# First edge attention of a four-layer graph network: the gathers of every fourth item wait for PE's shift of the maxima

## What is computed

```python
attn_score = jnp.sum(aw_q_edge * k[row_idx], axis=-1)      # one score for each edge and head
m = jax.ops.segment_max(score, col_idx, num_segments=n)
ex = jnp.exp(score - m[col_idx])
...
agg = jax.ops.segment_sum(alpha[..., None] * msg_edge, col_idx, num_segments=n)
```

## Time and profile before

| | |
|---|---|
| three runs | 6724.58, 6731.64, 6753.25 us; median 6731.64 us |
| span of the profiled execution, first to last instruction | 6706.8 us |
| its own time outside of the profiler | not given; the median of the runs lies 24.8 us above the span |
| busy: PE, DVE, POOL, ACT | 4342.6, 3458.5, 3192.9, 2184.9 us |
| first edge attention (l0e) | from about 619 to about 2280 us of the span |
| second edge attention (l3e) | from about 4884 to about 6572 us |

### The profile page before, as it was taken

The page is one execution under the profiler, slowest core; times in us unless marked ns, Lnnn a source line. Parts: engine busy times, 40 slices in busy tenths (PEclk is TensorE's granted clock), DMA queues, the critical chain, the costliest instruction groups (busy, mean ns, idle before and its releaser), DMA issues. The chain is left out here.

```text
span 6706.8 us, 90264 instructions
## 1 busy us (share of the span) xinstructions
PE 4342.6 (65%) x24913; PEld 3150.9 (47%) x24913; DVE 3458.5 (52%) x6689; ACT 2184.9 (33%) x7656; POOL 3192.9 (48%) x3187
## 2 busy tenths in 40 slices
PE   6996676766677744544444546887646666666676
PEld 4664454544445423333333435766335555555553
DVE  4452666666666662211111231112558888888885
ACT  1221455555545430000000111222225454555541
POOL 0422566666666236676676520002145565655551
PEclk8896777777777876666766778998778888888885
DMA  4334666666666525333333407882366666666673
GB/s 133 126 123 163 182 197 199 202 196 198 198 196 197 125 72 186 93 93 93 92 95 92 72 29 243 261 262 87 108 189 205 203 210 203 205 207 203 201 185 102
DMA packets 509932, 1077.03 MB, mean 161 GB/s; under 512 B 94770, under 2 KB 322388, under 8 KB 505993
## 3 DMA queue, kind: packets, MB, share of 16 engines
q0 software_dynamic: 204144, 617.42, 32.6%
q1 hardware_dynamic: 296854, 452.03, 20.2%
q10 hardware_dynamic: 8512, 2.74, 0.2%
HBM read 964.49 MB, written 194.54 MB: 173 GB/s over the span
## 5 line engine op out<-in xcount | busy, mean ns | idle before, releaser
L772 POOL DMA_INDIRECT l0e_kv<-t_table,k_recs x912 | 986.1, 1081 | 636.9 <-ACT l0e_vw L1049 375.5
L772 POOL DMA_INDIRECT l3e_kv<-t_table,k_recs x912 | 971.0, 1065 | 667.5 <-ACT l3e_vw L1049 368.0
L1464 PE MATMUL l2e_pA<-l2e_row,l2e_oh 128*128 128x257 f32 x1824 | 633.4, 516 | 768.7 <-issue 380.4
L1418 POOL DMA_INDIRECT l2e_row<-t_table,l2e_idx x912 | 899.7, 986 | 389.7 <-issue 265.4
L1464 PEld LDWEIGHTS l2e_pA<-l2e_row,l2e_oh 128*128 128x128 f32 x1824 | 460.0, 262 | 942.0 <-issue 852.9
L1006 PE MATMUL l0e_pA<-l0e_vw,l0e_ohf 128*128 128x260 f32 x1824 | 643.9, 500 | 198.3 <-ACT l0e_vw L1049 129.2
L958 PE MATMUL l3e_pQE<-l3e_qb,l3e_ohT 128*128 128x256 bf16 x2736 | 428.0, 318 | 405.9 <-issue 378.7
L1049 ACT ACTIVATE l3e_vw<-l3e_kv,l3e_w 128x64 f32<-128x64 f32 x2736 | 679.8, 334 | 0.0
L1049 ACT ACTIVATE l0e_vw<-l0e_kv,l0e_w 128x64 f32<-128x64 f32 x2736 | 679.6, 334 | 0.0
L1443 DVE SCALAR_TENSOR_TENSOR l2e_acc<-l2e_acc,k_itf,l2e_pA 128x257 f32<-128x257 f32 x228 | 109.9, 482 | 1058.6 <-issue 981.9
L1006 PEld LDWEIGHTS l0e_pA<-l0e_vw,l0e_ohf 128*128 128x128 f32 x1824 | 427.7, 247 | 338.5 <-ACT l0e_vw L1049 156.6
(11 more groups left out here) (469 smaller groups left out, 7126.8 us busy)
## 6 DMA issues: line engine op xcount, KB each, us to landing
exp_w<-in_L_gnn_w SPq DMA_DIRECT2D x224, 512.0 KB
t_table<-l0n_tab SPq DMA_DIRECT2D x26, 2048.0 KB, 6.9
l0e_qb<-t_q SPq DMA_DIRECT2D x228, 192.0 KB
l3e_qb<-t_q SPq DMA_DIRECT2D x228, 192.0 KB
t_agg<-l0e_acc SPq DMA_DIRECT2D x228, 130.0 KB
t_agg<-l3e_acc SPq DMA_DIRECT2D x228, 130.0 KB
l0e_drow<-t_drow SPq DMA_DIRECT2D x57, 512.0 KB
l3e_drow<-t_drow SPq DMA_DIRECT2D x57, 512.0 KB
```

Of the source, the lines that this page charges most:

```text
L772: pool.indirect_dma_start(kv[:, n % SK, g, :], None, table[:, :], bass.IndirectOffsetOnAxis(ap=K["recs"][:, n, g, ridx:ridx + 1], axis=0)) ...
L1418: pool.indirect_dma_start(row[:, s, g, 0:D], None, table[:, :], bass.IndirectOffsetOnAxis(ap=idx[:, i, g:g + 1], axis=0)).then_inc(row_rea ...
L1464: last = pe.matmul(pA[s % 2][:, 0:W], oh[:, s, g, :], row[:, s, g, :], start=(g == 0), stop=(g == G - 1))
```

## The change

Before the gathers of item n POOL gets one more wait, in the first edge attention alone, when n is 1 modulo 4 and over 8, so for n = 9, 13, ..., 225 (55 items):

```diff
                 if n >= SK:
                     pool.wait_ge(vwa_ready, n - SK + 1)
                     pool.wait_ge(vwd_ready, n - SK + 1)
+                if first and n % BI == 1 and n > 2 * BI:
+                    pool.wait_ge(sh_ps, (n - 1) // BI - 1)
                 for g in range(G):
```

## The result

The changed kernel is slower: 6857.62 us (6835.46 to 6870.38, four runs) against 6731.00 us of the kernel before beside it, a ratio of 1.0174 with a 95% interval of 1.0146 to 1.0202. By the ratio that is 117 us more, by the two medians 127 us, where 198 us less were forecast.

The account below looks back on a forecast made before the run. Bursts were taken as bound by PE's shift report, held until gathers drain. Release 0.1, 16 gathers 21.2, drain 3.0 and PE 0.3 make 24.6 us against 28.27, over 54 periods 198 us: 6731.6 - 198 = 6533 us, range 6463 to 6750.

Parts of the forecast that it names:

- What bounds the kernel: First edge attention: PE's report of the shift, awaited by `z`, is held while gathers stream; a burst takes 28.27 us.
- From report to last gather before the next hold this is the same 16 gathers, 21.2 us: POOL's part of the changed burst: four held gathers, then straight on with 12 more, 21.2 us of the 24.6 us.
- so it goes straight on with 12 more: POOL after the four held gathers: the next buffer is free by then, so 12 more gathers follow directly.
- The drain: End of the burst: the report comes once the last gathers run dry, 3.0 us after the last one starts.
- The 3.55 us: The drain by the skill's page instead of the trace: a burst 0.5 us longer, 27 us less gain in all.
- Rival (b): Report of `turn_ends` stuck until the held stream drains at 24.3 us: 29.8 us a burst, 6813 us; chance 0.11.
- in the usual burst it does arrive: Argument against (b): the report of `turn_ends` arrives in the usual burst although gathers stream by then.
- the upper end of 6750 us: Top of the forecast range, where rival (a) and a hold without effect lie; (b) is outside.
- The stream doesn't hold PE: Rival: shift's report comes 8 us late for a reason in PE; 6732 to 6772 us; no hold or effect 0.10.

Follow-up runs that it names:

- doubled shift: Kernel before with the shift's 16 small matmuls in the first attention made twice: 6724.94 us, ratio 1.0022; on another occasion 6061.19 us, ratio 0.9997.
- the first kernel with a wait for it: Kernel before, with `z` also waiting until the gathers of item 4m + 9 have landed: 6775.9 us, ratio 1.0089.
- late sessions: Four occasions on which the kernel before took 6716.51, 6714.36, 6749.65 and 6704.95 us, like the 6731 of the result.
- prompt sessions: Two occasions on which the kernel before took 6061.63 and 6064.69 us; in their profiles PE's reports are never late.
- the prompt timeline above: Timeline about one `z` of the changed kernel, unedited, run where the kernel before took 6064.69 us: 6062.0 us, ratio 0.9995.

## Why the prediction was wrong

**What bounds the kernel: right.** The burst was bound by a report of PE that hangs until the gathers drain. The wait of POOL is seen (166.0 us in 50 waits), the held gathers leave with `z`, and the report of the shift is prompt once the stream in front of it stops: 1.39 us from record to `z` (1533.36 to 1534.75), against 1.03 in the earlier trace rows. The doubled shift shows that more than half of what PE needs there was hidden, though not all.

**"From report to last gather before the next hold this is the same 16 gathers, 21.2 us": this step failed.** It measured 26.00 us (1504.11 to 1530.11). The 21.22 us of the earlier trace rows started 4.36 us behind `z`, and in those 4.36 us POOL issued nothing: the report of the sums for the third widening came at 1523.97, 8.07 us behind `z`, with three gathers of the new stream issued. With the hold the stream starts at `z`, and the same report waits out 12 gathers and the drain, 17.26 us; the weighing, the buffers and the last item's gathers wait for it. The prediction took the buffers for free ("so it goes straight on with 12 more"). POOL went on with 8 more, 12 in all, and then stood idle for 7.08 us, which the sum had at nothing: 14.17 + 3.09 + 4.93 + 3.81 us make the 26.00. It did not ask whose reports fall under the new stream.

**The drain** was sized rightly, 3.09 us against 3.03, but is paid in another place, in the middle of the burst, and at its end there are 4.64 us more instead of 3.3. Landing is a little later than the report: 3.85 us in the first kernel with a wait for it. The 3.55 us that had been estimated by the Trainium skill (DMA: Bandwidth & Descriptors, "Anatomy of one DMA") lie between the two.

**Rival (b) was the nearest to what happened**: another report stuck until the stream drains, a burst of 29.8 us and 6813 us, where 29.93 us (30.29 by the count of the earlier trace rows) and 6857.62 us were measured. That its burst came so near is in part luck, as its sum goes through another wait. It named the wrong report, `turn_ends` instead of the sums, and was given 0.11 because "in the usual burst it does arrive". That argument looked at one report and not at all those that come under the new stream. Its place in the range was lost with it: the upper end of 6750 us left out the very mechanism on which the forecast rested, applied to the next report in line.

**"The stream doesn't hold PE"** is refuted for the late sessions, where the remote waits shrink with the length of the stream, and is what the prompt sessions show: there the change gives 0.9995. The page that the Trainium skill has for it (SBUF — State Buffer, its opening lines) says that the ports cannot contend. The run with half the bytes agrees, in that traffic is not what matters; the held reports, and the matmuls of the doubled shift that start late under the stream, are outside of its rule.

**What stays open.** What delays PE is not shown. The doubled shift shows that PE's matmuls themselves start late under the stream, so a late report may be no more than late work, but not what they wait for, nor what differs between the sessions; the granted clock, the chip and the bytes are excluded as its cause. POOL's issuing and the transfers behind it were not told apart by an experiment; the sums' report at 1521.37 came 2.14 us after POOL's last gather instruction had ended (1518.28 + 0.95), with transfers still under way up to it. That PE catches up in the 4.36 us without gathers, and needs them, is read from the timelines.

## What to carry to other kernels

If a report of one engine hangs while another streams transfers, a hold only moves the stream; list every report that falls under it in its new place, and ask of each who stands behind it. A burst time taken from the trace contains the pauses ahead of it that made it possible, so that "the same 16 gathers" take longer where a pause is gone. And time such a change on more than one occasion: here it costs 1.7% or nothing, while the kernel before itself takes 6731 or 6062 us.

## What was unexpected of the hardware

The same kernel takes 6062 us in some sessions and 6705 to 6750 us in others, on one chip in both, with gathers that take POOL 0.95 us in both (the earlier trace rows and the prompt timeline above). Reports of PE that come 8 to 10 us after the modelled end in the one come within 0.65 us of the recorded start in the other, in the middle of a stream. In the late sessions they come when gathers pause, some 3 to 4 us after the start of the last one, several in one instant (1521.37), with the bytes playing no part (124 or 198 GB/s). PE's small matmuls start late under such a stream as well, with idle times of 0.66 to 1.23 us between them where a prompt session has none (doubled shift). A gather that DVE's 2.28 us one-hot instruction meets takes 2.77 us. And a wait of POOL for its own gathers leaves it idle for 3.9 us in the mean: its next gather starts 4.3 to 5.8 us after the start of the last one, while a report comes 3.1 us after it.
